# A five-stage kernel on one core: the last stage's five experts, moved between GpSimd, VectorE and ScalarE

## The chip, the cores and the metric

The kernel runs on one core of a Trainium2 chip. The metric is the device time of one execution in microseconds (us). Before the change it is 247.75 us, the median of three runs (247.38 to 247.79).

A core has a matrix engine (TensorE, PE in the profile, with its weight loads apart as PEld), and three others that work beside it: VectorE (DVE), ScalarE (ACT) and GpSimd (POOL). Each works through its own list of instructions in the order in which they stand. They meet at semaphores only.

## The reference

Two batches of 128 rows of 512 numbers pass three blocks, each of which is added to its input: a cross-attention block with a feed-forward part, an RWKV block, and an attention block whose values are made by experts. The change concerns the last. Cut to what matters, with `h` = 8 heads, `e` = 5 experts and `dh` = 64:

```python
q = (x @ Wq), k = (x @ Wk)                     # per head, 64 wide
gl_v = (x @ Ws).reshape(b, t, h, e)
wv = _topk_mask(gl_v, 2) * sigmoid(gl_v)       # two of five experts for each row and head
xv = einsum('btd,edk->btek', x, Wv)            # five rows of 64 for each row of x
v = einsum('bthe,btek->bhtk', wv, xv)          # sum over the experts, for each head
probs = softmax(q k^T / 8)
attn = probs @ v
mask_o = _topk_mask((x @ Wd), 2)
out = einsum('bthe,bthk,ekd->btd', mask_o, attn, Wo)
```

So a batch's values are a sum of five products: for expert `e`, a row of 64 numbers (`xv`) is repeated for eight heads and multiplied by that head's gate (`wvm`).

## The kernel before

One program, five lists of instructions, no loops on the chip. Every producer counts up a semaphore, and a class `Flag` (L33) turns names into counts: `inc` marks a step done, `at` gives the count to wait for. As the names of a flag have to be raised in the order in which they are listed, a change of order in a list shows in them. TensorE's order is written out at the end of its block; so are VectorE's, ScalarE's and GpSimd's. Batches 0 and 1 alternate.

In the last stage (from about 200 us) the order on TensorE is: `fg(0)` (gates and expert rows), `fk(0)`, `fq(0)`, the transposes of batch 1's input, `score_f(0, 0)`, `fg(1)`, `fq(1)`, `score_f(0, 1)`, `fk(1)`, `turn_p0(1)`, `turn_p0(0)` (transposes of batch 0's weights), `score_f(1, 1)`, `score_f(1, 0)`, `av(0, 0)`, `av(0, 1)` (weights times values), `turn_max(1)` (the transpose of batch 1's maxima, L615), `score_t(1)`, `less_max(1)`, and from there the sums and the output matmuls of both batches. The scores of batch 1 are computed twice: `score_f(1, .)` only for the maxima, `score_t(1)` already transposed. From the latter `less_max(1)` subtracts the maxima, which is why it needs `turn_max(1)`. All matmuls are recorded at L398, all transposes of 128 columns at L402.

VectorE's part, for each batch: `logits` (L1090, copies 80 gate numbers out of PSUM), `ranks` (which two of five), `value_gate` (L1111), then `expert(b, e, first)`: a product (L1120) and, for all but the first, an addition to `N4[b]` (L1123). `values` (L1128) adds what GpSimd made and writes the values for `av`. `max_f(b, q)` (L1133) takes the row maxima of four heads from PSUM as soon as `score_f(b, q)` has written them; for batch 0 a small scaling (L1139) follows, and ScalarE's `exp_p0(q)` waits for that. `max_parts(1)` (L1150, L1152) splits batch 1's maxima in two parts, and `turn_max(1)` on TensorE waits for the second. `p0_turned` (L1144) copies half of batch 0's turned weights out of PSUM. After them stand `out_gate` and `gate_out` (L1158 to L1177), which prepare the sums, and `final` (L1181).

ScalarE's part: `expert_rows(b)` (copies `xv`, tanh for the gates), `fk_out`, `fq_out` (keys and queries out of PSUM, wanted by the scores), `copy_turned`, `exp_p0(q)`, `p0_turned` (the other half of the turned weights). All its operations have one line, L1440.

GpSimd's part: experts 3 and 4 of each batch (L1740) and their sum (L1849 for batch 0, L1853 for batch 1), after the eight small powers `deviation` (L1724) that the norms want.

Of the kernel before, what the change touches and what calls it, by code (L numbers as in the profile page):

```python
# [7 lines left out]
ALU = mybir.AluOpType  # L8
ACT = mybir.ActivationFunctionType
# [67 lines left out]
def build(nc, blocks, xin, vecs, cols, out):  # L77
    with ExitStack() as ctx:
# [3 lines left out]
        def sem(name):  # L82
            return ctx.enter_context(nc.semaphore(name))
# [20 lines left out]
        ones = sb("ones", [128, 128])  # L104
# [5 lines left out]
        v, a, g, t = nc.vector, nc.scalar, nc.gpsimd, nc.tensor  # L110
# [13 lines left out]
        def slot(i, n=1, of=slots):  # L124
            return of[:, i, :] if n == 1 else of[:, i:i + n, :].rearrange("p a n -> p (a n)")
# [4 lines left out]
        def heads(ap):  # L130
            return ap.rearrange("p (h k) -> p h k", h=8)

        def over(ap, n):
            return ap.unsqueeze(2).broadcast_to([128, ap.shape[1], n])
# [4 lines left out]
        def bank(n):  # L139
            return psum[:, n, :]  # L140
# [22 lines left out]
        R = [[18, 19, 20, 21, 26, 27, 28, 29], [22, 23, 24, 25, 30, 31, 32, 33]]  # L163
# [5 lines left out]
        x2b = [slot(36), slot(37)]  # L169
        MIX = [[slot(12), slot(14)], [slot(13), slot(15)]]  # L170
        kt = [slot(R[b][0]) for b in range(2)]
        vt = [slot(36), slot(R[1][2])]
        th = [slot(R[b][3]) for b in range(2)]
        km = [slot(2), slot(R[1][4])]
        ys = [slot(R[b][6]) for b in range(2)]
        sc_ = [slot(R[b][7]) for b in range(2)]
        w1, kx, c2t = slot(37), slot(3), slot(5)
# [41 lines left out]
        def flags(name, *orders):  # L219
            return [Flag(sem(f"{name}{b}"), orders[b if len(orders) > 1 else 0]) for b in range(2)]  # L220
# [30 lines left out]
        rk_v = flags("rwkv_dve", ["c", "km", "vc", "ys", "ss", "sb", "e", "pv", "y", "yb", "yg"], ["c", "rn", "km",  # L251
                     "ys", "c3", "c1", "sb", "c2s", "vc", "ss", "e", "pv", "yg"])
        gates_v = flags("gates_dve", ["gl", "mask", "w"])
        smax_v = flags("maxima_dve", ["0", "1", "turned"], ["1", "0", "high", "low"])
        val_v = flags("values_dve", ["vv"])
        out_v = flags("out_dve", ["ms0", "ms1", "0", "2", "1", "fin"], ["ms0", "ms1", "0", "1", "2", "fin"])

# [10 lines left out]
        by_a = flags("by_head_act", ["pv", "sc"], ["sc", "pv"])  # L268
        silu_a = flags("silu", ["tanh"])
        gates_a = flags("gates_act", ["xv", "w", "k", "q"], ["xv", "w", "q", "k"])  # L270
        exp_f = flags("exp_f", ["0", "1"])
        p_out0 = Flag(sem("weights_turned_act"), ["0"])
        mT_a = Flag(sem("max_turned_act"), ["mT"])
        sel_a = Flag(sem("select_act"), ["pick", "sel"])
        uT_a = flags("uT_act", ["0", "2", "1"], ["0", "1", "2"])
# [7 lines left out]
        x2b_g = flags("x2b", ["x2b"])  # L283
        mixed_g = Flag(sem("mixed_pool"), ["w", "g"])
        rk_g = flags("rwkv_pool", ["sb", "rs"], ["kx", "c2", "a", "w", "sb", "cov", "rs"])
        exp_g = flags("experts_pool", ["ones", "vv"])

        turn = flags("turn", TURNS)
        prod = flags("product", ["q1", "k1", "v1", "e1", "n1", "em", "pv", "q2", "k2", "n2", "v2", "f1", "f2", "a",
# [104 lines left out]
        def _(eng):  # L394
# [231 lines left out]
            def av(b, q):  # L626

                s.wait_ge(*val_v[b].at("vv"))
                s.wait_ge(*exp_g[b].at("ones"))
                if b:  # L630
                    s.wait_ge(*exp_f[1].at(str(q)))
                    s.wait_ge(*mT_a.at("mT"))
                else:
                    s.wait_ge(*(smax_v[0].at("turned") if q else p_out0.at("0")))
                    s.wait_ge(*exp_f[0].at("1"))
                for c in range(4):
                    i = mm(psum[:, 4 * b + (3 if q else 1), c * 65:(c + 1) * 65],
                           PTf[b][:, (4 * q + c) * 128:(4 * q + c + 1) * 128], VV[b][:, 2 * c + q, :], True, True)
                i.then_inc(*av_t[b].inc(str(q)))
# [173 lines left out]
        def _(eng):  # L813
# [274 lines left out]
            def logits(b):  # L1088
                s.wait_ge(*prod[b].at("fg"))
                v.tensor_copy(gl[b], psum[:, 4 * b + 2, 0:80]).then_inc(*gates_v[b].inc("gl"))  # L1090
# [23 lines left out]
            def expert(b, e, first):  # L1114
                x_ = xv[b][:, 0:320].rearrange("p (e k) -> p e k", e=5)[:, e, :].unsqueeze(1).broadcast_to([128, 8, 64])
                w_ = over(wvm[b].rearrange("p (h e) -> p h e", e=5)[:, :, e], 64)
                s.wait_ge(*gates_a[b].at("xv"))
                s.wait_ge(*gates_v[b].at("w"))
                s.wait_ge(*own_v.now())
                v.tensor_tensor(heads(N4[b] if first else Y[b]), x_, w_, ALU.mult).then_inc(*own_v.inc())  # L1120
                if not first:
                    s.wait_ge(*own_v.now())
                    v.tensor_tensor(N4[b], N4[b], Y[b], ALU.add).then_inc(*own_v.inc())  # L1123

            def values(b):
                s.wait_ge(*exp_g[b].at("vv"))
                s.wait_ge(*own_v.now())
                v.tensor_tensor(VV[b][:, :, 0:64], heads(vv[b]), heads(N4[b]), ALU.add).then_inc(  # L1128
                    *val_v[b].inc("vv"))

            def max_f(b, q):
                s.wait_ge(*sf[b].at(str(q)))
                i = v.tensor_reduce(mxf[b][:, 4 * q:4 * q + 4], quarters(4 * b + (1 if q else 3)), AX.X, ALU.max)  # L1133
                if b:
                    i.then_inc(*smax_v[1].inc(str(q)))
                else:
                    i.then_inc(*own_v.inc())
                    s.wait_ge(*own_v.now())
                    v.tensor_scalar(nmx[:, 4 * q:4 * q + 4], mxf[0][:, 4 * q:4 * q + 4], -0.125, None,  # L1139
                                    ALU.mult).then_inc(*smax_v[0].inc(str(q)))  # L1140

            def p0_turned():
                s.wait_ge(*sf[0].at("turn1"))
                v.tensor_copy(PTf[0][:, 512:1024], bank(2)).then_inc(*smax_v[0].inc("turned"))  # L1144

            def max_parts(b):

# [250 lines left out]
            expert(0, 1, False)  # L1398
            max_f(0, 0)
            expert(0, 2, False)  # L1400
            logits(1)
            values(0)
            ranks(1)
# [1 line left out]
            expert(1, 0, True)  # L1405
            max_f(0, 1)
            expert(1, 1, False)
            p0_turned()
            expert(1, 2, False)
            max_f(1, 1)  # L1410
            max_f(1, 0)
            max_parts(1)
            out_gate(0, 0)
# [22 lines left out]
        def _(eng):  # L1436
            s = Waits(eng)

            def act(o, x, func, **kw):
                return a.activation(o, x, func, **kw)  # L1440
# [108 lines left out]
            def expert_rows(b):  # L1549
                s.wait_ge(*gates_v[b].at("gl"))  # L1550
                act(xv[b][:, 0:320], psum[:, 4 * b + 2, 80:400], ACT.Copy, scale=0.5).then_inc(*gates_a[b].inc("xv"))
                act(wvm[b], gl[b][:, 0:40], ACT.Tanh, scale=0.5).then_inc(*gates_a[b].inc("w"))

            def fq_out(b):
                s.wait_ge(*prod[b].at("fq"))
                act(bcols(T10, b), quarters(4 * b + 3), ACT.Copy).then_inc(*gates_a[b].inc("q"))

            def fk_out(b):
                s.wait_ge(*prod[b].at("fk"))
                act(bcols(T16, b), quarters(4 * b), ACT.Copy).then_inc(*gates_a[b].inc("k"))  # L1560
# [18 lines left out]
            def exp_p0(q):  # L1579

                s.wait_ge(*smax_v[0].at(str(q)))
                for c in range(4):
                    n = 4 * q + c
                    i = act(P0[:, n * 128:(n + 1) * 128], psum[:, 1 if q else 3, c * 128:(c + 1) * 128], ACT.Exp,
                            bias=nmx[:, n:n + 1], scale=0.125)
                i.then_inc(*exp_f[0].inc(str(q)))

            def p0_turned():
                s.wait_ge(*sf[0].at("turn0"))
                act(PTf[0][:, 0:512], bank(0), ACT.Copy).then_inc(*p_out0.inc("0"))  # L1590

            def u_out(b, c):
                n = 64 if c == 2 else 128
# [100 lines left out]
            silu(1)  # L1694
            expert_rows(0)
            fk_out(0)
            fq_out(0)
            copy_turned(1, "n5", T8, 5)
            exp_p0(0)
            expert_rows(1)  # L1700
            exp_p0(1)
            fq_out(1)
            fk_out(1)
            p0_turned()
            max_turned(1)
            exp_p(1, 0)
            exp_p(1, 1)
# [10 lines left out]
        def _(eng):  # L1718
# [12 lines left out]

            def mul(o, x, y, flag, name, op=ALU.mult):
                g.tensor_tensor(o, x, y, op).then_inc(*flag.inc(name))  # L1733

            def expert(b, e, dst):
                x_ = xv[b][:, 0:320].rearrange("p (e k) -> p e k", e=5)[:, e, :].unsqueeze(1).broadcast_to([128, 8, 64])
                w_ = over(wvm[b].rearrange("p (h e) -> p h e", e=5)[:, :, e], 64)
                s.wait_ge(*gates_v[b].at("w"))
                s.wait_ge(*gates_a[b].at("xv"))
                return g.tensor_tensor(heads(dst), x_, w_, ALU.mult)  # L1740

            g.memset(mhalf[:, :], -0.5).then_inc(*const.inc("mhalf"))
            g.iota(kidx4[:, :], pattern=[[1, 512]], base=0, channel_multiplier=512,
# [99 lines left out]
            deviation(0, "n5")  # L1843
            deviation(1, "s")
            deviation(1, "n5")
            expert(0, 3, vv[0]).then_inc(*own_g.inc())
            expert(0, 4, vt2[0]).then_inc(*own_g.inc())
            s.wait_ge(*own_g.now())
            g.tensor_tensor(vv[0], vv[0], vt2[0], ALU.add).then_inc(*exp_g[0].inc("vv"))  # L1849
            expert(1, 3, vv[1]).then_inc(*own_g.inc())  # L1850
            expert(1, 4, vt2[1]).then_inc(*own_g.inc())
            s.wait_ge(*own_g.now())
            g.tensor_tensor(vv[1], vv[1], vt2[1], ALU.add).then_inc(*exp_g[1].inc("vv"))  # L1853


# [44 lines left out]
```

## Time and profile before

| | us |
|---|---|
| median of three runs | 247.75 (247.38 to 247.79) |
| the profiled execution | 247.14 |
| its span, first to last instruction | 245.4 |
| TensorE busy | 226.6 (92%) |
| VectorE busy | 162.7 (66%) |
| ScalarE busy | 92.8 (38%) |
| GpSimd busy | 75.5 (31%) |
| granted TensorE clock, mean | 0.993 of full speed |

The profile is one execution taken by the hardware profiler. Its page has the busy time of each engine, and the chain of work that ended last. The trace behind it can be asked for a timeline (instructions in order of time; neighbours of one kind are merged, with their count), for waits, and for busy times in stretches. In a timeline the brackets tell how long the engine had been idle before the instruction, and what ended the idle time. Durations of merged instructions run from the first start to the last end, so that instructions which overlap show as less than the sum of single ones.

### The profile page before, as it was taken

What the parts mean: (1) busy time and instruction counts of PE and PEld (TensorE: products, weight loads), DVE (VectorE), ACT (ScalarE), POOL (GpSimd) and SP (SyncE); (2) the same over time, 40 slices, a digit from 0 to 9 for tenths busy, and PEclk for the clock granted to TensorE, in tenths of its full rate; (3) what the DMA queues carried; (4) which work ended last, traced back from release to release, by engine and by line L of the source; (5) the groups of instructions that cost most, each with busy time, mean ns of one, the idle gap of its engine ahead of it and who ended that gap; (6) DMA issues with size and microseconds to landing.
All of it is one profiled execution on the core that took longest, in us unless ns stands there. A gap on an engine that the chain in (4) does not pass through costs nothing.

```text
span 245.4 us, 3036 instructions
## 1 busy us (share of the span) xinstructions
PE 226.6 (92%) x1136; PEld 159.0 (65%) x1136; DVE 162.7 (66%) x314; ACT 92.8 (38%) x175; POOL 75.5 (31%) x74
## 2 busy tenths in 40 slices
PE   5899999999899999979988999999898689999994
PEld 5878778798688777648463444444343269799951
DVE  2036454757768995990481754989975769988971
ACT  2152041447278769402106226267501221322210
POOL 4052021106508652341140204375215314260000
PEclk9999999999799999999999999999999999999999
DMA  7999995069944977186600079940000000000001
GB/s 256 419 429 408 441 402 214 1 236 427 371 170 168 386 300 282 61 341 236 280 0 0 0 206 421 425 192 0 0 0 0 0 3 0 1 4 0 3 30 55
DMA packets 6351, 43.99 MB, mean 179 GB/s; under 512 B 832, under 2 KB 832, under 8 KB 1472
## 3 DMA queue, kind: packets, MB, share of 16 engines
q1 hardware_dynamic: 6336, 43.80, 44.9%
q8 instruction: 9, 0.15, 0.2%
q14 instruction: 6, 0.05, 0.1%
HBM read 43.27 MB, written 0.52 MB: 178 GB/s over the span
## 4 chain that ended last, share of the span: by engine, by line
PE 80%; DVE 9%; ACT 4%; issue 3%; POOL 2%; DVEq 0%; POOLq 0%
PE psum L398 76%; PE psum L402 4%; ACT slots L1440 3%; DVE small L817 2%; POOL small L1724 2%; DVE ring_r L841 1%; PE psum L515 1%; DVE slots_r L943 1%; ACT ring_r L1440 1%; DVE slots L835 1%; DVE slots L957 1%; DVE small L819 0%; DVE slots L825 0%; ACT slots_r L1440 0%; DVE small L821 0%
## 5 line engine op out<-in xcount | busy, mean ns | idle before, releaser
L398 PE MATMUL psum<-ring,slots 128*128 128x512 f32 (+3 forms) x228 | 90.5, 546 | 5.0 <-ACT slots L1440 5.0
L398 PEld LDWEIGHTS psum<-ring,slots 128*128 128x128 f32 (+1 forms) x228 | 39.4, 190 | 46.3 <-issue 35.4
L1440 ACT ACTIVATE slots<-psum 128x512 f32<-128x512 f32 (+3 forms) x43 | 22.8, 543 | 90.8 <-PE psum L398 51.1
L398 PE MATMUL psum<-slots,ring 128*128 128x128 f32 x448 | 52.7, 277 | 2.3 <-ACT slots L1440 2.3
L398 PEld LDWEIGHTS psum<-slots,ring 128*128 128x128 f32 x448 | 51.3, 192 | 4.2 <-ACT slots L1440 3.2
L398 PE MATMUL psum<-ring_r,slots_r 128*128 128x512 f32 x192 | 48.7, 407 | 1.7 <-DVE slots_r L943 1.7
L398 PEld LDWEIGHTS psum<-ring_r,slots_r 128*128 128x128 f32 x192 | 36.1, 194 | 11.6 <-DVE slots_r L943 2.6
L1729 POOL TENSOR_TENSOR ring_r<-ring,ring_r 128x640 fp32r<-128x640 f32 x16 | 30.8, 1934 | 36.1 <-ACT ring_r L1440 36.1
L1440 ACT ACTIVATE ring_r<-ring 128x2048 fp32r<-128x2048 f32 (+1 forms) x17 | 31.6, 1865 | 12.9 <-PE psum L398 8.3
L1724 POOL TENSOR_TENSOR small<-small,mhalf 128x1 f32<-128x1 f32 x16 | 12.7, 795 | 77.1 <-DVE small L821 77.1
L841 DVE TENSOR_TENSOR ring_r<-ring,ring_r 128x1408 fp32r<-128x1408 f32 x16 | 28.4, 1786 | 5.8 <-ACT ring_r L1440 5.8
L402 PE MATMUL psum<-ident,slots 128*128 128x128 f32 x104 | 15.7, 282 | 2.5 <-DVE slots L825 1.8
L402 PEld LDWEIGHTS psum<-ident,slots 128*128 128x128 f32 x104 | 12.1, 143 | 9.0 <-DVE slots L825 2.9
L817 DVE BATCH_NORM_STATS2 small<-slots 128x6 f32<-128x512 f32 x16 | 11.1, 694 | 10.1 <-DMA slots<-xin 9.7
L1440 ACT ACTIVATE slots<-psum,small 128x128 f32<-128x128 f32 (+1 forms) x12 | 6.7, 615 | 13.7 <-DVE small L1139 7.5
L1733 POOL TENSOR_TENSOR slots<-slots,bc 128x512 f32<-128x512 f32 x5 | 6.4, 1272 | 17.3 <-ACT slots L1440 9.8
L398 PE MATMUL psum<-slots 64*128 64x128 f32 (+2 forms) x68 | 9.9, 300 | 0.2 <-ACT slots L1440 0.2
L835 DVE SCALAR_TENSOR_TENSOR slots<-slots,small,bc 128x512 f32<-128x512 f32 x10 | 7.5, 750 | 3.8 <-POOL small L1724 3.8
L1440 ACT ACTIVATE slots_r<-psum 128x512 fp32r<-128x512 f32 (+1 forms) x11 | 6.2, 566 | 8.7 <-PE psum L398 4.1
L398 PEld LDWEIGHTS psum<-slots 64*128 64x128 f32 (+1 forms) x68 | 7.6, 188 | 1.4 <-issue 0.6
L1440 ACT ACTIVATE slots<-slots,small 128x128 f32<-128x128 f32 x22 | 7.0, 390 | 3.3 <-DVE small L882 3.2
L957 DVE SCALAR_TENSOR_TENSOR slots<-psum,small,slots 128x512 f32<-128x512 f32 x2 | 1.5, 750 | 10.1 <-PE psum L398 10.1
(165 smaller groups left out, 205.0 us busy)
## 6 DMA issues: line engine op xcount, KB each, us to landing
ring<-blocks SPq DMA_DIRECT2D x36, 1024.0 KB, 8.3
bc<-vecs SPq DMA_DIRECT2D x1, 3072.0 KB, 28.6
bc<-vecs SPq DMA_DIRECT2D x1, 1280.0 KB, 7.0
slots<-xin SPq DMA_DIRECT2D x2, 256.0 KB, 6.1
bc<-vecs SPq DMA_DIRECT2D x1, 512.0 KB, 21.8
y<-slots SPq DMA_DIRECT2D x2, 256.0 KB, 2.0
colv<-cols SPq DMA_DIRECT2D x1, 14.0 KB, 7.1
```

The lines of the kernel that those rows point to most:

```text
L398: return t.matmul(o_, l, r, start=first, stop=last)
L402: i = t.transpose(o_[:, c * 128:(c + 1) * 128], x[:, c * 128:(c + 1) * 128], ident[:, :])
L515: i = t.matmul(bank(4 * b + n), pick_r[:, n, :], pen_r[b], start=False, stop=True, skip_group_check=True)
L817: v.bn_stats(st[b], x).then_inc(*own_v.inc())
L835: v.scalar_tensor_tensor(out=o, in0=tmp, scalar=rs[b], in1=vec(bname), op0=ALU.mult, op1=ALU.add).then_inc(*normed[b].inc(name))
L841: v.tensor_tensor(ring_r[:, p, 0:CUT], ring[:, p, 0:CUT], ring_r[:, high(name), 0:CUT], ALU.subtract).then_inc(*split_low.inc(name))
L943: v.tensor_tensor(Em_r[b][:, at_], bank(4 * b + n % 2), PT_r[b][:, at_], ALU.subtract).then_inc(*p_low[b].inc(str(n)))
L957: v.scalar_tensor_tensor(out=Y[b], in0=bank(4 * b), scalar=rv2[b], in1=Z[b], op0=ALU.mult, op1=ALU.add).then_inc(*y_in[b].inc("2"))
L1440: return a.activation(o, x, func, **kw)
L1724: g.tensor_tensor(rs[b], ve[b], mhalf[:, 0:1], ALU.pow).then_inc(*rstd[b].inc(name))
L1729: g.tensor_tensor(ring_r[:, p, CUT:], ring[:, p, CUT:], ring_r[:, high(name), CUT:], ALU.subtract).then_inc(*split_lowg.inc(name))
L1733: g.tensor_tensor(o, x, y, op).then_inc(*flag.inc(name))
```

## The change

GpSimd's `expert` and the six instructions that used it are taken out. Expert 3 of both batches goes to VectorE, as a fourth call of its `expert`: for batch 0 behind `max_f(0, 0)` and expert 2, for batch 1 between `max_f(1, 1)` and `max_f(1, 0)`. Expert 4 goes to ScalarE, as eight activations of 64 columns, one for each head, with the head's gate as scale. They stand before `fq_out(0)` for batch 0, and between `expert_rows(1)` and `exp_p0(1)` for batch 1. They write where `values` reads (`vv`). VectorE's `p0_turned` is gone; ScalarE's does both halves, half 1 first.

```diff
-        smax_v = flags("maxima_dve", ["0", "1", "turned"], ["1", "0", "high", "low"])
+        smax_v = flags("maxima_dve", ["0", "1"], ["1", "0", "high", "low"])
+        exp_a = flags("experts_act", ["4", "3"][:1])
-        p_out0 = Flag(sem("weights_turned_act"), ["0"])
+        p_out0 = Flag(sem("weights_turned_act"), ["1", "0"])
-        exp_g = flags("experts_pool", ["ones", "vv"])
+        exp_g = flags("experts_pool", ["ones"])
...
@@ TensorE, av @@
-                    s.wait_ge(*(smax_v[0].at("turned") if q else p_out0.at("0")))
+                    s.wait_ge(*p_out0.at(str(q)))
@@ VectorE @@
             def values(b):
-                s.wait_ge(*exp_g[b].at("vv"))
+
+                s.wait_ge(*exp_a[b].at("4"))
...
-            def p0_turned():
-                s.wait_ge(*sf[0].at("turn1"))
-                v.tensor_copy(PTf[0][:, 512:1024], bank(2)).then_inc(*smax_v[0].inc("turned"))
...
             expert(0, 1, False)
             max_f(0, 0)
             expert(0, 2, False)
+            expert(0, 3, False)
             logits(1)
             values(0)
             ranks(1)
...
             expert(1, 0, True)
             max_f(0, 1)
             expert(1, 1, False)
-            p0_turned()
             expert(1, 2, False)
             max_f(1, 1)
+            expert(1, 3, False)
             max_f(1, 0)
             max_parts(1)
@@ ScalarE @@
+            def expert(b, e):
+
+                s.wait_ge(*gates_v[b].at("w"))
+                s.wait_ge(*gates_a[b].at("xv"))
+                dst = vv[b] if e == 4 else vt2[b]
+                for h in range(8):
+                    i = act(dst[:, h * 64:(h + 1) * 64], xv[b][:, e * 64:(e + 1) * 64], ACT.Copy,
+                            scale=wvm[b][:, h * 5 + e:h * 5 + e + 1])
+                i.then_inc(*exp_a[b].inc(str(e)))
...
-            def p0_turned():
-                s.wait_ge(*sf[0].at("turn0"))
-                act(PTf[0][:, 0:512], bank(0), ACT.Copy).then_inc(*p_out0.inc("0"))
+            def p0_turned(q):
+                s.wait_ge(*sf[0].at(f"turn{q}"))
+                act(PTf[0][:, q * 512:(q + 1) * 512], bank(2 * q), ACT.Copy).then_inc(*p_out0.inc(str(q)))
...
             fk_out(0)
+            expert(0, 4)
             fq_out(0)
             copy_turned(1, "n5", T8, 5)
             exp_p0(0)
             expert_rows(1)
+            expert(1, 4)
             exp_p0(1)
             fq_out(1)
             fk_out(1)
-            p0_turned()
+            p0_turned(1)
+            p0_turned(0)
             max_turned(1)
@@ GpSimd @@
-            expert(0, 3, vv[0]).then_inc(*own_g.inc())
-            expert(0, 4, vt2[0]).then_inc(*own_g.inc())
-            s.wait_ge(*own_g.now())
-            g.tensor_tensor(vv[0], vv[0], vt2[0], ALU.add).then_inc(*exp_g[0].inc("vv"))
-            expert(1, 3, vv[1]).then_inc(*own_g.inc())
-            expert(1, 4, vt2[1]).then_inc(*own_g.inc())
-            s.wait_ge(*own_g.now())
-            g.tensor_tensor(vv[1], vv[1], vt2[1], ALU.add).then_inc(*exp_g[1].inc("vv"))
```

## Rows read from the trace of the kernel before

**Rows 1.** The page, busy us (share of the span) and instructions of each engine.

```profile
PE 226.6 (92%) x1136; PEld 159.0 (65%) x1136; DVE 162.7 (66%) x314; ACT 92.8 (38%) x175; POOL 75.5 (31%) x74
```

**Rows 2.** The chain that ended last, 205 to 245.4: start us, us, what.

```profile
208.14 0.61 ACT slots L1440
...
225.81 16.39 PE psum L398 x100
```

**Rows 3.** Timeline of GpSimd: start us, us, engine line op out<-in xcount.

```profile
216.16 2.58 POOL L1740 TENSOR_TENSOR slots<-slots,small 128x512 f32<-128x512 f32 x2 [5.72 <-DVE small L1111]
218.82 1.67 POOL L1853 TENSOR_TENSOR slots<-slots 128x512 f32<-128x512 f32 x1
```

**Rows 4.** Timeline of VectorE, 205 to 226.

```profile
205.74 0.20 DVE L1111 SCALAR_TENSOR_TENSOR small<-small 128x40 f32<-128x40 f32 x1
...
209.36 1.64 DVE L1123 TENSOR_TENSOR slots<-slots 128x512 f32<-128x512 f32 x1
210.92 0.68 DVE L1133 TENSOR_REDUCE small<-psum 128x4 f32<-128x512 f32 x1
...
213.03 0.23 DVE L1090 COPY small<-psum 128x80 f32<-128x80 f32 x1
...
217.52 0.69 DVE L1133 TENSOR_REDUCE small<-psum 128x4 f32<-128x512 f32 x1 [0.71 <-PE psum L398]
...
219.40 1.64 DVE L1123 TENSOR_TENSOR slots<-slots 128x512 f32<-128x512 f32 x1
221.73 0.69 DVE L1144 COPY slots<-psum 128x512 f32<-128x512 f32 x1 [0.69 <-PE psum L402]
222.34 0.68 DVE L1120 TENSOR_TENSOR slots<-slots,small 128x512 f32<-128x512 f32 x1
223.05 0.69 DVE L1123 TENSOR_TENSOR slots<-slots 128x512 f32<-128x512 f32 x1
...
225.18 0.17 DVE L1152 TENSOR_TENSOR slots_r<-small,slots_r 128x8 fp32r<-128x8 f32 x1
```

**Rows 5.** Timeline of TensorE, 205 to 232, and of its weight loads.

```profile
216.33 1.16 PE L398 MATMUL psum<-slots 64*128 64x128 f32 x8
...
222.06 1.71 PE L398 MATMUL psum<-slots 64*128 64x128 f32 x16
223.70 2.00 PE L398 MATMUL psum<-ring,slots 128*128 128x65 f32 x16
...
228.44 1.16 PE L398 MATMUL psum<-ident,ring 128*128 128x128 f32 x8
...
225.42 0.14 PEld L615 LDWEIGHTS psum<-ident,slots 128*16 128x16 f32 x1
```

**Rows 6.** Timeline of ScalarE at the copy that waits for 228.44, and VectorE's `max_f(1, 1)`.

```profile
229.63 0.28 ACT L1440 ACTIVATE slots<-psum 128x128 f32<-128x128 f32 x1 [0.48 <-PE psum L398]
...
223.66 0.68 DVE L1133 TENSOR_REDUCE small<-psum 128x4 f32<-128x512 f32 x1
```

**Rows 7.** Timeline of ScalarE, 205 to 224.

```profile
208.14 1.09 ACT L1440 ACTIVATE slots<-psum 128x512 f32<-128x512 f32 x2 [2.98 <-PE psum L398]
...
221.29 0.60 ACT L1440 ACTIVATE slots<-psum 128x512 f32<-128x512 f32 x1 [0.86 <-PE psum L398]
222.16 0.60 ACT L1440 ACTIVATE slots<-psum 128x512 f32<-128x512 f32 x1 [0.28 <-PE psum L402]
```

**Rows 8.** Timeline of ScalarE in the stage before: scaled copies and what follows them.

```profile
152.86 1.27 ACT L1440 ACTIVATE slots<-slots,small 128x128 f32<-128x128 f32 x4
154.03 0.58 ACT L1440 ACTIVATE psum<-psum 128x512 f32<-128x512 f32 x1
...
169.86 1.98 ACT L1440 ACTIVATE psum<-slots,small 128x64 f32<-128x64 f32 x8
```

**Rows 9.** Groups by line and form, ScalarE: busy us, mean ns of one.

```profile
L1440 ACT ACTIVATE psum<-slots,small 128x64 f32<-128x64 f32 x8 | 2.0, 296 | 0.0
```

**Rows 10.** Busy us (instructions) in a stretch: PE, PEld, DVE, ACT, POOL; clock; DMA.

```profile
184.00:192.00 8.00, 4.96 (x17) 2.29 (x15) 5.15 (x11) 2.49 (x4) 4.28 (x5) 1.00 0.00 0
```

More of the change, by code:

```diff
@@ L171, in build @@
         kt = [slot(R[b][0]) for b in range(2)]
+        rt = [slot(R[b][1]) for b in range(2)]
         vt = [slot(36), slot(R[1][2])]
@@ L174, in build @@
         km = [slot(2), slot(R[1][4])]
+        gt = [slot(R[b][5]) for b in range(2)]
         ys = [slot(R[b][6]) for b in range(2)]
@@ L1733, in mul @@
                 g.tensor_tensor(o, x, y, op).then_inc(*flag.inc(name))
[L1735 to L1740, printed above, removed]
             g.memset(mhalf[:, :], -0.5).then_inc(*const.inc("mhalf"))
```

## The prediction

> **What bounds the kernel now.** I read the page's busy line first: TensorE is busy for 92% of the span [rows 1]. An average does not say what the last stage is worth, so the second view is the chain of waits from 205 us on. It shows ScalarE for one piece of 0.61 us at 208.14 (the copy of the batch 0 query product) and TensorE for everything else: the last long piece runs without a break from 225.81 for 16.39 us, up to the last addition [rows 2]. A change to VectorE, ScalarE and GpSimd can then move the end in two ways only: by delaying something TensorE waits for, or by releasing it earlier where it waits now. So the third view is the timeline of each engine from 205 to 226 us, to find, for every wait of TensorE, how long its releaser had been done. The stage starts from a stream that is bound by TensorE and has three tight places: `fq_out(0)` at 208.14, `fk_out(1)` at 221.29 [rows 7], and `max_parts(1)`, whose last instruction ends at 225.18 + 0.17 = 225.35, 0.07 before the load for `turn_max(1)` (L615) at 225.42 [rows 4, 5].
>
> **Part 1: GpSimd's experts go.** GpSimd does two products in 2.58 us and a sum in 1.67 us for batch 1, and as much for batch 0 [rows 3]. Nobody waits for them: `values(0)` and `values(1)` come later in VectorE's own order. What they do cost is VectorE time. While GpSimd works, VectorE's additions of 128x512 take 1.64 us, at 209.36 and at 219.40, where the same addition takes 0.69 at 223.05 [rows 4]. So these two rows alone give back 2 x 0.95 = 1.9 us of VectorE.
>
> The Trainium skill (SBUF — State Buffer, section "SBUF: two separate sides") says that VectorE operations with two SBUF inputs and GpSimd operations exclude each other for a whole instruction. The addition at 219.40 agrees: it ends at 221.04, 0.55 after GpSimd's sum ended at 218.82 + 1.67 = 220.49, as if it had begun only then. By that rule alone one would expect a gain here; the parts below say why the sum has none.
>
> **Part 2: expert 3 of batch 0 on VectorE.** A product and an addition take 223.66 - 222.34 = 1.32 us together, start to next start [rows 4, 6]. Without GpSimd VectorE reaches `max_f(0, 0)` 0.95 or more before 210.92, by 209.97, and waits there for the scores. Two groups of eight matmul records (128 columns) show how long such a group takes to become readable: 216.33 to the maximum at 217.52, 1.19 us; and 228.44 to ScalarE's copy at 229.63, again 1.19 [rows 4, 5, 6]. `score_f(0, 0)` starts at 208.79 (the chain's 208.14 + 0.61, and the issue), so the maximum starts at 209.98 instead of 210.92, 0.94 earlier. Add the new pair: `logits(1)` moves by 1.32 - 0.94 = +0.38, from 213.03 to 213.41. The string from there to `max_f(0, 1)` had 0.71 of idle in front of 217.52, which swallows it. No cost; `max_f(0, 1)` stays at 217.52, since TensorE sets it.
>
> **Part 3: expert 4 on ScalarE, eight scaled copies of 64 columns each.** Such a copy with SBUF on both sides is not in the trace. The nearest row below is eight copies of 64 columns from SBUF to PSUM: 1.98 us for all. The nearest above is four of 128 columns from SBUF to SBUF, after which the next instruction starts 154.03 - 152.86 = 1.17 later, 0.29 each, so 2.34 for eight [rows 8]. For batch 0 the gate ends at 205.94 [rows 4], the copies start at about 205.97 and end between 207.95 and 208.31. Behind them on ScalarE stands `fq_out(0)`, ready at 208.14, and TensorE's `score_f(0, 0)` waits for that. Cost 0 to 0.17 us; I take 0, because the width and count of the 1.98 row are the same and only the destination differs. `copy_turned(1, "n5")`, next in the queue, is wanted only after eight more matmuls. For batch 1 the gate comes at 216.16 + 0.38 = 216.5 (GpSimd's release in rows 3) and the copies last to 218.5 or 218.9. Behind them stand `exp_p0(1)`, whose input now comes at about 218.4, `fq_out(1)`, and `fk_out(1)`, which had 0.86 idle ahead of 221.29 [rows 7]. Nothing of that is late. If this cover were gone, `fk_out(1)` would delay `score_f(1, 1)` one for one.
>
> The Trainium skill (ScalarE: Activation LUTs, section "Rules for kernel authors") speaks against this part: about 0.3 us per activation and 0.83 ns an element. By it, as an estimate, eight would take 8 x (0.3 + 0.053) = 2.8 us, and `fq_out(0)` would be 0.66 late. The rows measure 1.98 for eight, because successive ones overlap.
>
> **Part 4: both turned copies of batch 0 on ScalarE.** VectorE loses a copy of 0.69 us at 221.73 and the wait in front of it (0.69) [rows 4]. ScalarE, free at about 221.8 after `fk_out(1)`, takes half 1 and then half 0. Consecutive copies of 128x512 start 1.09 - 0.60 = 0.49 apart [rows 7], so half 0 is done at about 221.9 + 0.5 + 0.6 = 223.0 instead of 222.76. `av(0, 0)` starts behind the scores at 222.06 + 1.71 = 223.77, or just before [rows 5]; 0.7 us of cover. Cost 0.
>
> **Part 5: expert 3 of batch 1, put between the two maxima.** This decides. `max_f(0, 1)` starts at 217.52; with its 0.69 and a small scaling of about 0.17 (as at 225.18) VectorE is free at about 218.4, and experts 1 and 2 take it to 218.4 + 2 x 1.32 = 221.0. Even if none of the contention went away it would be 221.04 + 0.61 (1.32 less the 0.71 idle) + 1.32 = 223.0. Next in order is `max_f(1, 1)`, and its scores start at 222.06, released by `fk_out(1)` [rows 5, 7], which has not moved. They are readable at 222.06 + 1.19 = 223.25. In the kernel before VectorE arrived at 223.66 [rows 6], later than that, so no wait is seen. Now it stands idle for some 2 us, from 221.0 to 223.25, and only afterwards does it the new pair, with `max_f(1, 0)` and `max_parts(1)` queued behind. The end of `max_parts(1)` was 225.35 for a start of 223.66. Now it is 223.25 + (225.35 - 223.66) + 1.32 = 226.26, that is 0.91 later. `turn_max(1)` is next in TensorE's fixed order behind `av(0, 1)`, so TensorE stands still from 225.42 to 226.33, with `score_t(1)`, `less_max(1)` and all output matmuls behind it.
>
> **The sum.** VectorE's output gates stand behind `max_parts(1)` in its order and move by the same 0.91, so neither of the two streams can take it back: from 225.81 on TensorE is the chain's only piece [rows 2]. 0 + 0 + 0 + 0.91 = +0.9 us. The granted clock is 1.00 in a stretch in which TensorE is busy for only 4.96 of 8 us [rows 10], so I add nothing for the clock. Against the profiled execution's 247.14 us (span 245.4) that gives 248.05. The median of the runs is 247.75, 0.61 above the profiled one, so the forecast is 247.75 + 0.9 = 248.65.
>
> **The rivals.**
> (a) VectorE's time reaches the end: faster. For it speak the 1.9 us of contention and the 1.4 us of copy and wait against 2.6 us of new pairs. For `max_parts(1)` to be earlier at all, the scores must be readable before 223.66 - 1.32 = 222.34, 0.28 after their first matmul starts; the two groups measured took 1.19. And `turn_max(1)` can't pass `av(0, 1)`, whose matmuls start at 223.70. At most some tenths: 247.4.
> (b) No change that can be measured (0.2%, 0.5 us, is what a measurement of this kernel can tell apart). The scores are readable 0.4 or more before 223.25, or later slack takes part of the stall. TensorE's pieces after 225.8 hold few waits, so this gives 247.9 to 248.2.
> (c) Slower by more: ScalarE's copies of batch 0 overrun `fq_out(0)`. It decides from 0.27 us a copy on (2.17 us between 205.97 and 208.14). At 0.29 it adds 0.17, so 248.8. If they did not overlap at all, at the 0.296 us of a single one of 64 columns [rows 9], they would end at 208.34: +0.20. At the 1.27 / 4 = 0.32 of the wider copies from SBUF to SBUF [rows 8], 208.51: +0.37, 249.0.
>
> The Trainium skill's price named in part 3 lies beyond these: +0.66, 249.3.
>
> (d) The change does not do what it says, because VectorE's slow additions were not GpSimd's doing. Part 5 shows that VectorE is at the maximum in time even so; the result is the forecast again.
>
> **How the numbers follow.** Forecast with (d) 0.65, (c) 0.15, (b) 0.13, (a) 0.07. The range takes in the forecast, the copies' 0.17 and 0.37, and most of (b): 247.8 to 249.2. Faster 0.07; same 0.15 (most of (b), and forecasts that come out small); slower 0.78.
>
> **What the profile after should show.** VectorE's maximum of batch 1 (L1133's counterpart) idle for about 2 us ahead of it, released by a TensorE matmul; then a product and an addition of 0.7 each before the second maximum. The load of `turn_max` with about 0.9 us of idle, released by VectorE. All VectorE additions at 0.69. Eight scaled copies on ScalarE in some 2 us, ended by 208.1, with `fq_out(0)` still 0.02 behind TensorE. The times up to 222.06 as before. The prediction is wrong if the maximum starts with no idle, if `fq_out(0)` starts later than 208.2, or if TensorE's load at `turn_max` shows no wait.

## The result, and the profile after

| | before | changed |
|---|---|---|
| median of the runs, us | 247.77 (247.38 to 247.85, 4 runs) | 252.63 (251.01 to 257.16, 4 runs) |
| the profiled execution, us | 247.14 | 252.69 |
| its span, us | 245.4 | 251.0 |
| granted clock over the span | 0.993 | 0.973 |

The ratio is 1.0178, with a 95% interval of 1.0129 to 1.0227. The forecast was 248.65, in a range up to 249.2: the side was right, the size was not. All ratios leave out executions more than 1.5% above the fastest of their kernel, and these are mostly the ones with a long fall of TensorE's clock, so the mean clock of the executions is given beside the medians.

The page of the changed kernel, against [rows 1]: VectorE and GpSimd are busy for less time, ScalarE for 4.4 us more, TensorE for 4.9 us more with the same 1136 instructions. Under it stands the clock in 40 slices of 6.3 us, in tenths.

```profile
PE 231.5 (92%) x1136; PEld 163.5 (65%) x1136; DVE 161.4 (64%) x317; ACT 97.2 (39%) x192; POOL 67.3 (27%) x68
...
PEclk9999999999799999999999999999999999997599
```

The timeline of VectorE in the changed kernel, against [rows 4, 6] (start us, us, engine line op, count, idle before and its releaser). L1123 is the experts' product, L1126 their addition, L1137 the maximum, L1152 the last instruction of `max_parts`.

```profile
210.01 0.69 DVE L1137 TENSOR_REDUCE small<-psum 128x4 f32<-128x512 f32 x1 [1.53 <-PE psum L401]
...
217.55 0.69 DVE L1137 TENSOR_REDUCE small<-psum 128x4 f32<-128x512 f32 x1 [0.18 <-PE psum L401]
...
219.07 0.69 DVE L1126 TENSOR_TENSOR slots<-slots 128x512 f32<-128x512 f32 x1
...
223.28 0.69 DVE L1137 TENSOR_REDUCE small<-psum 128x4 f32<-128x512 f32 x1 [2.06 <-PE psum L401]
223.88 0.68 DVE L1123 TENSOR_TENSOR slots<-slots,small 128x512 f32<-128x512 f32 x1
224.60 0.69 DVE L1126 TENSOR_TENSOR slots<-slots 128x512 f32<-128x512 f32 x1
225.21 0.68 DVE L1137 TENSOR_REDUCE small<-psum 128x4 f32<-128x512 f32 x1
...
226.13 0.17 DVE L1152 TENSOR_TENSOR slots_r<-small,slots_r 128x8 fp32r<-128x8 f32 x1
```

The first maximum of batch 1 waits 2.06 us for TensorE and starts at 223.28; the new pair follows it, and `max_parts(1)` ends 0.95 later than in [rows 4]. Now TensorE in the same kernel, with the load of `turn_max(1)` (L618) first, against [rows 5].

```profile
226.35 0.09 PEld L618 LDWEIGHTS psum<-ident,slots 128*16 128x16 f32 x1 [0.77 <-DVE slots_r L1152]
```

```profile
226.56 1.71 PE L401 MATMUL psum<-slots 64*128 64x128 f32 x16
228.20 1.65 PE L401 MATMUL psum<-slots_r,ring_r 16*128 16x128 f32 x8
229.77 2.08 PE L401 MATMUL psum<-ident,ring 128*128 128x128 f32 x8
```

The load starts at 226.35 instead of 225.42, 0.93 later. `score_t(1)` takes 1.71 us as before. The third row is `sum_u(0, 0)`, 2.08 us long, where [rows 5] has 1.16 at 228.44. Nothing waits there; the engine is slower. The busy times by stretch of the changed kernel show it (stretch, length, then busy us of PE, PEld, DVE, ACT and POOL with their counts, granted clock, DMA share and GB/s).

```profile
227.00:228.00 1.00, 1.00 (x15) 1.00 (x13) 1.00 (x3) 0.00 (x0) 0.00 (x0) 1.00 0.00 0
228.00:229.00 1.00, 1.00 (x8) 0.88 (x7) 0.96 (x2) 0.00 (x0) 0.00 (x0) 0.79 0.00 0
229.00:230.00 1.00, 1.00 (x5) 0.88 (x6) 1.00 (x3) 0.72 (x2) 0.00 (x0) 0.50 0.00 0
...
238.00:239.00 1.00, 1.00 (x6) 1.00 (x6) 0.97 (x3) 0.00 (x0) 0.00 (x0) 0.59 0.00 0
239.00:240.00 1.00, 1.00 (x4) 0.41 (x3) 1.00 (x3) 0.28 (x1) 0.00 (x0) 1.00 0.00 0
```

From about 228.6 to 238.8 the granted clock is 0.50, the lower of the two levels (1.2 in place of 2.4 GHz). In the kernel before it was 1.00 over the same part of the stage:

```profile
226.00:237.00 11.00, 11.00 (x77) 8.54 (x77) 10.72 (x24) 2.02 (x6) 0.00 (x0) 1.00 0.01 1
```

The chain of the changed kernel (start us, us, what) has the same 100 matmuls as [rows 2], but they take 21.13 us instead of 16.39.

```profile
226.63 21.13 PE psum L401 x100
247.76 0.02 issue
247.78 0.69 DVE slots L1181
```

The account: the last addition starts at 247.78 instead of 242.21, 5.57 later. Of this 0.93 is the later start of the load for `turn_max(1)`. The rest, 4.64, is the way from that load to the last addition, 21.43 us instead of 16.79, with the same instructions, of which 10.2 us pass at the lower clock.

### The profile page after: what moved, and what is told of

It reads as the page before. It is cut to its first block, busy times and chain, and to the rows that moved or that the text cites. A ratio compares the mean times of both kernels' runs of the same rounds, so it can differ in the third digit from the quotient of the medians.

```text
span 251.0 us, 3050 instructions
## 1 busy us (share of the span) xinstructions
PE 231.5 (92%) x1136; PEld 163.5 (65%) x1136; DVE 161.4 (64%) x317; ACT 97.2 (39%) x192; POOL 67.3 (27%) x68
## 4 chain that ended last, share of the span: by engine, by line
PE 80%; DVE 10%; ACT 4%; issue 3%; POOL 2%; DVEq 0%; POOLq 0%
PE psum L401 75%; PE psum L405 4%; ACT slots L1441 3%; DVE small L820 2%; POOL small L1738 2%; DVE ring_r L844 1%; PE psum L518 1%; DVE slots_r L946 1%; ACT ring_r L1441 1%; DVE slots L838 1%; DVE slots L960 1%; DVE small L1137 1%; DVE small L822 0%; DVE slots L828 0%; ACT slots_r L1441 0%
## 5 line engine op out<-in xcount | busy, mean ns | idle before, releaser
L401 PE MATMUL psum<-ring,slots 128*128 128x512 f32 (+3 forms) x228 | 92.1, 556 | 5.0 <-ACT slots L1441 5.0
L401 PEld LDWEIGHTS psum<-ring,slots 128*128 128x128 f32 (+1 forms) x228 | 41.2, 200 | 46.3 <-issue 35.4
L820 DVE BATCH_NORM_STATS2 small<-slots 128x6 f32<-128x512 f32 x16 | 11.1, 694 | 10.2 <-DMA slots<-xin 9.7
L1441 ACT ACTIVATE slots<-slots,small 128x128 f32<-128x128 f32 (+1 forms) x38 | 11.1, 367 | 6.3 <-DVE small L885 3.2
L401 PEld LDWEIGHTS psum<-ident,ring 128*128 128x128 f32 (+1 forms) x48 | 7.8, 233 | 2.1 <-issue 1.8
L401 PE MATMUL psum<-ident,ring 128*128 128x128 f32 (+1 forms) x48 | 9.1, 358 | 0.0
```

What stands on the lines that cost most here:

```text
L401: return t.matmul(o_, l, r, start=first, stop=last)
L820: v.bn_stats(st[b], x).then_inc(*own_v.inc())
```

## The experiments

The theory after the comparison: the pair between the maxima makes TensorE stand still for most of a microsecond (0.77 in the trace), in a stretch in which its work is light (matmuls on 64 and 16 rows, or of 65 columns, in place of 128 by 128 and more), and this lets the clock fall for some 10 us. The rivals: the fall comes from another part of the change (ScalarE's copies, the missing GpSimd work); it comes with any wait of this size, wherever; it is the lateness and not the standing still; it belongs to the chip.

The start of this stage moves by almost 4 us between the profiled executions for things ahead of it, so each reading below is of the wait in front of `turn_max(1)` and of the clock behind it, not of absolute positions. "Long falls" are executions with a mean clock of 0.98 or less. The kernel before had 4 of these in the 71 executions that stood beside the experiments (2 of 19, 0 of 23, 2 of 29); the changed kernel had them in 8 of 8, over two comparisons. A mean clock tells how much of an execution ran low, not where: one fall of 10.2 us alone gives 0.98, and three of 3.4 us give the same. Only the profiled execution of each kernel shows the place.

**e1: the pair ahead of both maxima.** Only the place of expert 3 of batch 1 changes, into VectorE's idle time.

```diff
             expert(1, 2, False)
+            expert(1, 3, False)
             max_f(1, 1)
-            expert(1, 3, False)
             max_f(1, 0)
```

> The changed kernel with one line moved: expert 3 of batch 1 stands ahead of max_f(1, 1) instead of behind it, in VectorE's idle 2 us. Theory (the pair between the maxima makes TensorE stand still, and this makes the clock fall): max_f(1, 1) still starts at 223.3, turn_max(1) has no wait, the clock stays 1.00 from 226 on, 247.4 to 247.9 us. Rival (another part of the change, the copies on ScalarE or the missing GpSimd work, lowers the clock): 251 to 253 us with the clock at 0.50 somewhere after 226.

Measured: 247.84 us (10 runs, 245.40 to 251.43) against 247.03, ratio 1.0018 (0.9973 to 1.0062). Weight loads and VectorE in e1:

```profile
223.71 0.14 PEld L618 LDWEIGHTS psum<-ident,slots 128*16 128x16 f32 x1
```

```profile
221.53 1.29 DVE L1137 TENSOR_REDUCE small<-psum 128x4 f32<-128x512 f32 x2 [0.61 <-PE psum L401]
```

Both maxima run one behind the other, the load of `turn_max` has no idle in front of it, and the clock is 1.00 over the whole span; two of the ten executions had a long fall (0.977 and 0.979), against two of 19 beside them. So the rest of the change is not what lowers the clock. With everything but one line as in the changed kernel, this also says what the other parts are worth: nothing that can be measured, between 0.3% less and 0.6% more.

**e2: the wait filled with full matmuls.** The changed kernel, late as it is, but TensorE has work meanwhile.

```diff
             av(0, 1)
+            for _ in range(4):
+                mm(psum[:, 0, 0:128], ones[:, :], ones[:, :], True, True)
             turn_max(1)
```

> The changed kernel with four more matmuls of 128x128 (ones by ones, into a free part of PSUM) on TensorE ahead of turn_max(1): eight records, about 0.86 us, just the length of the wait. Theory (it is TensorE's standing still that makes the clock fall): the clock stays 1.00, the lateness of 0.9 us is all that is left, 248.5 to 248.9. Rival (the clock falls because the thin matmuls of this stage come later, or because of what the other engines do): 251 to 253 as in the changed kernel.

Measured: 248.74 us (10 runs) against 247.03, ratio 1.0047 (1.0004 to 1.0090); one long fall in ten. The eight records in front of `turn_max`, and the clock behind (PE busy, clock, DMA share, GB/s):

```profile
226.37 0.97 PEld L401 LDWEIGHTS psum<-ones 128*128 128x128 f32 x8
227.26 0.09 PEld L618 LDWEIGHTS psum<-ident,slots 128*16 128x16 f32 x1
```

```profile
230.00:232.00 2.00, 2.00 (x19) 1.00 0.00 0
```

TensorE is as late as in the changed kernel (its load comes 2.67 us behind the start of `av(0, 0)`, there 2.63) and keeps its clock. So the lateness by itself does not lower it. What remains, 1.2 us with an interval of 0.1 to 2.2, agrees with the 0.9 of the forecast.

**e3 and e4: the wait without the change.** The kernel before, with GpSimd's experts and all else in place, and one (e4) or two (e3) additional VectorE operations of 128x512 between the maxima, writing scratch space (a helper in the kernels, written out here in its place).

```diff
             max_f(1, 1)
+            s.wait_ge(*own_v.now())
+            for _ in range(n):                      # n = 2 in e3, 1 in e4
+                v.tensor_tensor(Y[1], N4[1], N4[1], ALU.mult).then_inc(*own_v.inc())
+                s.wait_ge(*own_v.now())
             max_f(1, 0)
```

> The kernel before (GpSimd's experts and all else in place) with two additional VectorE operations of 128x512 between max_f(1, 1) and max_f(1, 0), which write scratch space: about 1.4 us. Theory: TensorE waits about 1.4 us at turn_max(1), the clock falls to 0.50 behind it for some us, 252 to 254. Rival (the fall belongs to another part of the change): only the wait, 249.1 to 249.3, clock 1.00.

> The kernel before with one additional VectorE operation in that place, about 0.7 us. Theory: a wait of 0.6 to 0.7 us at turn_max(1); the delay alone gives 248.4, and if a standstill of this size is enough for the clock, 251 to 252.5. Rival (the fall belongs to another part of the change): 248.4, clock 1.00.

Measured: e3 253.06 us (4 runs), ratio 1.0217 (1.0160 to 1.0273); e4 252.94 us (4 runs), ratio 1.0198 (1.0115 to 1.0282). Long falls in all eight. The load of `turn_max`, e3 and then e4, each with the clock behind:

```profile
227.56 0.09 PEld L615 LDWEIGHTS psum<-ident,slots 128*16 128x16 f32 x1 [1.30 <-DVE slots_r L1158]
```

```profile
230.00:232.00 2.00, 2.00 (x10) 0.50 0.00 0
```

```profile
224.37 0.09 PEld L615 LDWEIGHTS psum<-ident,slots 128*16 128x16 f32 x1 [0.57 <-DVE slots_r L1158]
```

```profile
228.00:229.00 1.00, 1.00 (x7) 0.50 0.00 0
```

One operation of 0.7 us on VectorE costs this kernel some 5 us. The wait alone, with none of the change, brings the whole effect, and 0.57 us bring nearly as much as 1.30.

**e9: a smaller dose.** As e4, with 128 columns in place of 512.

```diff
             max_f(1, 1)
+            s.wait_ge(*own_v.now())
+            v.tensor_tensor(Y[1][:, 0:128], N4[1][:, 0:128], N4[1][:, 0:128], ALU.mult).then_inc(*own_v.inc())
+            s.wait_ge(*own_v.now())
             max_f(1, 0)
```

> The kernel before with a third of the additional work of e4 between the maxima (128 columns, about 0.3 us). Theory (the stage stands close to the point where the clock falls, so the longer the standstill, the more of the executions fall for long): a wait of 0.3 us at turn_max(1); some executions at 248.0 with the clock at 1.00, some with a fall of a few us, median 248.5 to 251. Rival (a standstill of that size is harmless): 248.0 to 248.2 and not more spread than the kernel before.

Measured: 248.69 us (11 runs, 246.46 to 253.03) against 247.35, ratio 0.999 (0.9945 to 1.0036) over the six without a long fall. Five of the eleven have a long fall (mean clock 0.970 to 0.980, 250.9 to 253.0 us); the other six are at 0.983 (one), 0.993 (two) and 1.000 (three). The profiled one fell, behind a wait of 0.17 us:

```profile
226.62 0.09 PEld L615 LDWEIGHTS psum<-ident,slots 128*16 128x16 f32 x1 [0.17 <-DVE slots_r L1152]
```

```profile
230.00:232.00 2.00, 2.00 (x12) 0.50 0.00 0
```

With 4 in 71, 5 in 11 and 4 in 4 for no addition, 0.3 us and 0.7 us, a longer wait makes the long fall more frequent. The middle count is small, and of its five only the profiled one shows that the fall stands behind this wait.

**e5: the wait filled with matmuls of 16 rows.** e2 again; only the operands' rows differ.

```diff
+            for _ in range(4):
+                mm(psum[:, 0, 0:128], ones[0:16, :], ones[0:16, :], True, True)
             turn_max(1)
```

> The changed kernel with the wait at turn_max(1) filled as in e2, but by matmuls whose operands have 16 rows instead of 128. Theory (it is the standing still that counts): as e2, clock 1.00 behind it, 248 to 249. Rival (rows count too: work on few rows does not hold the clock as work on 128 rows does): the clock at 0.50 for some us behind 228, 251 to 253 us.

Measured: 251.89 us (4 runs) against 247.71, ratio 1.0169 (1.0118 to 1.0219); long falls in three of four. Loads and clock in e5:

```profile
227.55 0.96 PEld L401 LDWEIGHTS psum<-ones 16*128 16x128 f32 x8
228.63 0.09 PEld L618 LDWEIGHTS psum<-ident,slots 128*16 128x16 f32 x1
```

```profile
230.00:232.00 2.00, 2.00 (x12) 0.64 0.00 0
232.00:234.00 2.00, 2.00 (x9) 0.50 0.04 8
```

My own expectation was wrong here. The eight records last 0.96 us, as the full ones do (0.97), no idle is shown in front of `turn_max`, and the profile counts TensorE as busy in the same way, yet the clock falls. The number of rows makes the difference: filled on 128 rows the wait left one long fall in ten, filled on 16 rows three in four (on different chips, each beside the kernel before). So it is not the standing still as such; a wait and work on few rows act alike.

**e6: the pair behind `max_parts(1)`.** Now the wait is moved to the far side of the light stretch, ahead of `sum_u(0, 0)`.

```diff
             max_f(1, 1)
-            expert(1, 3, False)
             max_f(1, 0)
             max_parts(1)
+            expert(1, 3, False)
             out_gate(0, 0)
```

> The changed kernel with expert 3 of batch 1 behind max_parts(1), ahead of the output gates. turn_max(1) then has no wait, but VectorE's output gates stand about 1.3 us behind (0.8 us later than TensorE can use them), so that TensorE waits some 0.8 us ahead of sum_u(0, 0). Theory (a standstill of this size in this stage lowers the clock wherever it lies): the clock at 0.50 behind it, 250 to 253. Rival (only a standstill ahead of the thin matmuls score_t and less_max does it): 0.8 us and no more, 248 to 249.

Measured: 252.58 us (4 runs), ratio 1.0212 (1.0170 to 1.0254); long falls in all four. Loads and clock in e6:

```profile
226.10 0.96 PEld L401 LDWEIGHTS psum<-slots_r,ring_r 16*128 16x128 f32 x8
227.92 1.78 PEld L401 LDWEIGHTS psum<-ident,ring 128*128 128x128 f32 x8 [0.86 <-DVE ring L1177]
```

```profile
227.00:228.00 1.00, 0.28 (x3) 0.77 0.00 0
228.00:229.00 1.00, 1.00 (x5) 0.50 0.00 0
```

Here the clock falls while TensorE is still standing. Ahead of the matmuls of 64 and 16 rows (0.77 us) or behind them (0.86 us), a wait has the same effect.

**e7: a wait between full matmuls.** e1, with four more scaled copies on ScalarE ahead of `fq_out(0)`, so that TensorE waits at 208 between long runs of matmuls with 128 rows (one group of eight records of 64 rows stands directly behind the wait).

```diff
+                if b == 0:
+                    for h in range(4):
+                        act(vt2[b][:, h * 64:(h + 1) * 64], xv[b][:, e * 64:(e + 1) * 64], ACT.Copy,
+                            scale=wvm[b][:, h * 5 + e:h * 5 + e + 1])
                 i.then_inc(*exp_a[b].inc(str(e)))
```

> The kernel of e1 (pair ahead of the maxima) with four more scaled copies of 64 columns on ScalarE ahead of fq_out(0): about 1 us, of which 0.8 is visible, so TensorE stands still for about 1.3 us ahead of score_f(0, 0) at 208, between long runs of matmuls with 128 rows. Theory (few-row matmuls around the standstill are needed too): the delay of 0.8 alone, clock 1.00 throughout the last stage, e1's time + 0.8. Rival (any standstill of more than half a us lowers the clock): clock at 0.50 for some us behind 210, e1's time + 3 or more.

Measured: 247.62 us (10 runs) against 247.71, ratio 1.0024 (0.9993 to 1.0055), no long fall. Load and clock in e7:

```profile
209.34 0.96 PEld L401 LDWEIGHTS psum<-slots 64*128 64x128 f32 x8 [1.18 <-ACT slots L1441]
```

```profile
210.00:214.00 4.00, 4.00 (x21) 1.00 0.00 0
```

The wait is 1.18 us, more than in the changed kernel (it was 0.49 in e1), and in the profile the clock does not move behind it. The mean clocks of the ten (0.992 to 1.000) leave room for one short fall each, not for a long one. The interval, -0.2 to +1.4 us, holds the 0.7 by which the wait grew and leaves out the 3 or more of the rival. Together with e5 this says that a wait is expensive where the work around it is light; that nothing else about the place at 208 protects it was not tried.

**e8 and e10: the first fall filled.** The profile of the kernel before has a fall of its own, from 65 to 68.4 us. This is its stretch at that place, and TensorE's timeline ahead of it:

```profile
63.00:64.00 1.00, 0.07 (x1) 1.00 0.95 401
64.00:65.00 1.00, 1.00 (x4) 1.00 0.93 300
65.00:66.00 1.00, 1.00 (x3) 0.50 0.97 361
```

```profile
63.93 1.19 PE L515 MATMUL psum<-slots_r 4*128 4x512 f32 x4 [0.99 <-DVE slots_r L931]
```

It is the same picture: 0.99 us without work, then matmuls of 4 rows. e8 is e1, and e10 the kernel before, with this:

```diff
             count2(0)
+            for _ in range(4):
+                mm(psum[:, 4, 0:128], ones[:, :], ones[:, :], True, True)
             shut_out(0)
```

> The kernel of e1 with four more matmuls of 128x128 (ones by ones) between count2(0) and shut_out(0), where TensorE stands still for 0.99 us at 63 us and the clock fell to 0.50 from 65 to 68.6 in the profiles of the kernel before and of the changed one, ahead of matmuls with 4 rows. Theory (the same cause as in the last stage): no fall at 65, about 1.7 us less than the kernel before in the executions in which that one has the fall, 245.5 to 246.5. Rival (the fall there has another cause, or the fill delays what follows): as e1, 247 to 248.

> The kernel before with the four matmuls of e8 between count2(0) and shut_out(0) and nothing else. Theory (standing still 1 us ahead of four-row matmuls makes the clock fall at 65): no fall there, 1 to 1.7 us faster than the kernel before where that one has the fall; the median 0.3 to 1.5 us lower. Rival (TensorE's extra matmuls delay the rest by what the clock gives back): within 0.2%.

Measured: e8 246.99 us (12 runs) against 247.71, ratio 0.9985 (0.9953 to 1.0017); e10 246.62 us (12 runs) against 247.35, ratio 0.9995 (0.9963 to 1.0027). Neither gain is clear of the noise. In both profiles the clock is 1.00 from 60 to 70. But each fell somewhere else for 3.4 us: e8 at 228 with no wait ahead of `turn_max`, e10 at 192.5, at the end of the idle stretch that starts at 190. First e8, then e10:

```profile
228.00:229.00 1.00, 1.00 (x7) 0.63 0.00 0
```

```profile
190.00:192.00 2.00, 0.00 (x0) 1.00 0.00 0
192.00:194.00 2.00, 1.41 (x2) 0.64 0.00 0
```

The gap at 190 is 2.65 us long in every one of these kernels and lies between matmuls on 128 rows; here is TensorE behind it in the kernel before, where the clock stayed at 1.00:

```profile
192.29 3.70 PE L398 MATMUL psum<-ring,slots 128*128 128x512 f32 x8 [2.65 <-ACT slots L1440]
```

Five of the fourteen profiles (e3, e6, e9, e10, e12) show a fall of 3.4 us that begins in the last half microsecond of this gap. So full rows around a gap do not keep the clock up whatever its length: they did at 1.18 us in e7, and not always at 2.65.

The kernel has several such places, and one execution falls at one, the next at another. Not counting those that the end of the span cuts off, the falls in the fourteen profiles have two lengths only: twelve last 3.4 us, and the seven behind a wait or a 16-row fill in the last stage last 10.2. The one in that stage without a wait, in e8, is a short one.

Of the twelve profiles of kernels without the fill, six show a fall that starts between 64 and 67, of the two with it none. The mean clocks point the same way: none of the 24 executions with the fill is below 0.989, against 16 of the 52 of the kernel before that stood beside them. The fill's effect on the fall is thus likely, but as the time did not follow it is not called shown.

**e11 and e12: e1 and the changed kernel side by side.**

> The kernel of e1 again, beside the kernel before and the changed one on the same chip. Theory (without the wait at turn_max(1) the change costs and gives nothing that TensorE sees): within 0.3% of the kernel before. Rival (VectorE's freed time reaches the end): 0.3 to 1 us faster.

> The changed kernel as it is, on the same chip as e11. Theory: 3.5 to 5.5 us above e11, of which 0.9 is the wait and the rest 10 us at half the clock; the clock near 0.97 in every execution. Rival (the fall of the clock is a property of the chip of the first comparison): 0.9 us above e11.

Measured, against 247.35 for the kernel before: e11 247.11 us (12 runs, 245.44 to 248.69), ratio 0.9993 (0.9958 to 1.0028), no long fall; e12 253.56 us (4 runs), ratio 1.0214 (1.0154 to 1.0274), long falls in all four, one of them at a mean clock of 0.950. The distance between the two is 6.5 us, more than expected. The 0.9 us and one long fall do not make it up: the four mean clocks (0.950 to 0.970) are all below the 0.98 of one long fall alone, and the profiled one has a short fall at 190 beside the long one. The wait in e12 is the same as in the first profile:

```profile
225.08 0.09 PEld L618 LDWEIGHTS psum<-ident,slots 128*16 128x16 f32 x1 [0.77 <-DVE slots_r L1152]
```

No version beats the kernel before by more than the measurement can tell.

## Why the prediction was wrong, point by point

- **Part 1, GpSimd's hold on VectorE: right.** The addition that took 1.64 us takes 0.69 (219.07), and all others with it. The agreement claimed there is close, not exact: the addition at 219.40 ended 0.55 us after GpSimd's sum, where a whole one takes 0.69.
- **Part 2: right.** The maximum was forecast for 209.98 and started at 210.01; the one at 217.52 came at 217.55. Between them `logits(1)` came at 213.59 instead of 213.41, which the idle time ahead of 217.55 swallowed but for 0.18.
- **Part 3: right in its choice.** ScalarE in the changed kernel:

```profile
206.00 2.02 ACT L1441 ACTIVATE slots<-slots,small 128x64 f32<-128x64 f32 x8 [0.81 <-DVE small L1114]
208.17 1.09 ACT L1441 ACTIVATE slots<-psum 128x512 f32<-128x512 f32 x2
```

  The eight copies take 2.02 us, beside 1.98 in the row chosen and 2.34 at the upper bound, and `fq_out(0)` starts 0.03 later than before. Rival (c) is out, and with it the estimate of 2.8 us from the Trainium skill (ScalarE: Activation LUTs, "Rules for kernel authors"), which adds single activations up; here successive ones start 0.25 us apart.
- **Part 4: right.** `av(0, 0)` starts at 223.72 (223.70 before).
- **Part 5: right to the last step.** 2.06 us idle against "some 2 us", 223.28 against 223.25, the load at 226.35 against 226.33. Its idle is 0.77 and not "about 0.9", as it counts from the end of the loads of `av(0, 1)` at 225.58 and not from 225.42.
- **The sum: the step that failed is the clock.** The text says "I add nothing for the clock", on the ground of one stretch in which TensorE was busy for 4.96 of 8 us at a clock of 1.00 [rows 10]. That term was not 0 but 4.64 us, five times the forecast's only other one. The row could not carry this. It shows one execution, and that was luck: in five of the fourteen profiles the clock fell at the end of the long gap in that row. It also shows matmuls of 128 rows by 512 columns around its gap, whereas the stretch in question has 64 rows, 16 rows and 65 columns; e2 against e5 shows that rows count, and e7 against e4 and e6 that a wait among full rows can be harmless where a shorter one among few rows is not. The mechanism up to the load of `turn_max(1)` was right; what was put at nothing is what that wait does to the clock behind it.
- The row that bears on it was in the profile of the kernel before, at 63 to 66 us: 0.99 us of standing still, matmuls of 4 rows, then 0.50. The page's clock line has one slice below the others there, and the prediction did not ask what TensorE had done ahead of it.
- **Rivals.** (a), VectorE's freed time reaches the end, is refuted for the changed kernel by its ratio. With the wait gone as well, e1 and e11 lie between -0.3 and +0.6% and between -0.4 and +0.3% of the kernel before, too wide to exclude the some tenths of a microsecond that (a) spoke of, but VectorE still waits 0.61 us for TensorE ahead of the maxima there. (b) is out. (d) is out, since the additions became fast. None of the four had the clock in it, so the range ended at 249.2. That a wait costs its own length and no more was an assumption of all of them.

What stays open: whether the number of columns counts like the rows do, why a fall lasts 3.4 us in some places and 10.2 in others, how long a wait among full rows may be, and what in an execution decides whether a place such as those at 65 and 190 falls. None of this was tried.

## What to carry to other kernels

Before a wait is put on TensorE at its length, look at the rows of the matmuls on both sides of it, and look up in the kernel's own trace what stood ahead of every fall of the clock. Where the work is light, half a microsecond of delay on an engine that seemed to have slack can cost 5 us. One stretch of one execution with the clock at 1.00 does not show that a gap is harmless; look at the same place in several profiles. When work is moved onto an engine with idle time, put it into the idle time: here the same pair costs nothing that can be measured one line further up.

## What was not expected of the hardware

- A wait of 0.57 us (e4) between matmuls of 128x65, 64x128 and 16x128 brought the clock from 1.00 to 0.50 for 10.2 us in the profile, and the mean clocks of all 4 executions (0.970 to 0.977) fit that; with a wait of 0.17 us in the profile (e9) 5 of 11 do. A wait of 1.18 us between long runs of 128 rows (e7) brought no long fall in 10.
- TensorE busy with 16-row matmuls for the whole of the wait (e5) lost the clock in the same way in 3 of 4 executions; with 128-row ones of equal duration (e2) there was no long fall in 9 of 10. The busy share in the profile shows no difference between them.
- After the fall in the changed kernel TensorE was busy without a break, at the lower level, for 10.2 us before the clock came back. In e8 a fall in the same part of the stage, with no wait ahead of it, lasted 3.4 us.
- A gap of 2.65 us between matmuls on 128 rows ended in a fall of 3.4 us in 5 of 14 profiles, of kernels that do not differ there.
